# Down-projection weight tiles issued from ScalarE's DMA queue instead of SyncE's

## What is computed

```python
x = x.reshape(8, 256, 1024)          # 2048 tokens
# adapter: per batch entry, 16 ranks, indices itok_B_2_6
gate = x @ W_gate.T + 0.5 * (x @ A_gate[i].T) @ B_gate[i].T     # 2752 wide
up   = x @ W_up.T   + 0.5 * (x @ A_up[i].T)   @ B_up[i].T
act  = silu(gate) * up
down = act @ W_down.T + 0.5 * (act @ A_down[i].T) @ B_down[i].T # 1024 wide
x = x + down
x = x + (x @ weight.T + bias + scale[j] * (x @ lora_a[j].T) @ lora_b[j].T)
```

## Time and profile before

| | |
|---|---|
| time, median of 3 runs | 1600.11 us (1598.25 to 1603.44) |
| profiled execution | 1601.35 us, its span 1599.6 us |
| TensorE matmul busy | 1563.7 us, 98% |
| VectorE, GpSimd, ScalarE busy | 66%, 61%, 37% |
| TensorE's granted clock over the span | 0.995 |

### The profile page before, as it was taken

The page is one execution under the profiler, slowest core; times in us unless marked ns, Lnnn a source line. Parts: engine busy times, 40 slices in busy tenths (PEclk is TensorE's granted clock), DMA queues, the critical chain, the costliest instruction groups (busy, mean ns, idle before and its releaser), DMA issues.

```text
span 1599.6 us, 20865 instructions
## 1 busy us (share of the span) xinstructions
PE 1563.7 (98%) x6820; PEld 1275.6 (80%) x6820; DVE 1056.7 (66%) x1047; ACT 599.1 (37%) x1042; POOL 971.3 (61%) x679
## 2 busy tenths in 40 slices
PE   6999999999999999999999999999999999999998
PEld 4878888888888788888888877888787887778886
DVE  5786666666777877667677766474747546855433
ACT  3744444444445544444444422223232324431010
POOL 5577767766674777677666766767575644641110
PEclk9999999999999999999999999999999999999999
DMA  8334544533443355345552475444435242203322
GB/s 162 102 109 129 168 116 129 168 102 103 144 126 102 93 167 179 107 127 184 130 126 87 163 238 132 119 112 120 125 102 137 84 122 76 60 18 82 82 54 53
DMA packets 290878, 189.54 MB, mean 118 GB/s; under 512 B 164692, under 2 KB 252756, under 8 KB 290388
## 3 DMA queue, kind: packets, MB, share of 16 engines
q1 hardware_dynamic: 229424, 124.23, 30.7%
q10 hardware_dynamic: 61220, 63.98, 12.1%
q0 software_dynamic: 128, 0.00, 0.0%
HBM read 133.08 MB, written 56.46 MB: 118 GB/s over the span
## 4 chain that ended last, share of the span: by engine, by line
PE 85%; SPq 3%; DVE 3%; issue 3%; POOL 3%; DMA 2%; ACT 1%; DVEq 0%; ACTq 0%; POOLq 0%
PE ps L2447 85%; SPq L1477 1%; SPq L612 1%; POOL W L2223 1%; DMA x_first<-in_x_dram 1%; DMA turned_w<-in_L_cond_W_down_dram 1%; SPq L1434 1%; ACT Bf L1789 0%; DVE acc L1156 0%; DMA last_landed<-act_scratch 0%; DVE TG L663 0%; POOL Ws_S L2321 0%; POOL Bf L2306 0%; POOL act_last L2361 0%; SPq L1406 0%
## 5 line engine op out<-in xcount | busy, mean ns | idle before, releaser
L2447 PE MATMUL ps<-X_T,W 128*128 128x512 f32 x1944 | 458.0, 390 | 5.7 <-POOL W L2223 2.5
L2447 PE MATMUL ps<-X_B,W 128*128 128x512 f32 x1728 | 418.6, 392 | 14.3 <-ACT X_B L1717 13.1
L2447 PEld LDWEIGHTS ps<-X_T,W 128*128 128x128 f32 x1944 | 365.2, 188 | 84.4 <-issue 6.5
L2447 PEld LDWEIGHTS ps<-X_B,W 128*128 128x128 f32 x1728 | 326.5, 189 | 84.0 <-issue 14.6
L2223 POOL TENSOR_TENSOR W<-s,W 128x512 fp32r<-128x512 f32 x156 | 228.0, 1470 | 56.0 <-ACT W L1688 53.2
L1131 DVE TENSOR_TENSOR acc<-acc,ps 128x1024 f32<-128x1024 f32 x140 | 168.2, 1214 | 125.6 <-PE ps L2447 125.5
L2314 POOL TENSOR_TENSOR moving<-landed,moving 128x1024 fp32r<-128x1024 f32 x70 | 172.3, 2471 | 122.0 <-ACT moving L1942 122.0
L2447 PE MATMUL ps<-moving,Ws_S 128*128 128x512 f32 x960 | 222.1, 391 | 4.1 <-DVE acc L1131 2.8
L2447 PEld LDWEIGHTS ps<-moving,Ws_S 128*128 128x128 f32 x960 | 180.8, 189 | 44.0 <-issue 5.1
L2223 POOL TENSOR_TENSOR W<-TG,W 128x512 fp32r<-128x512 f32 x88 | 124.8, 1419 | 123.8 <-ACT W L1688 123.6
L1688 ACT ACTIVATE W<-s 128x512 fp32r<-128x512 f32 x156 | 98.5, 633 | 226.8 <-PE ps L2447 198.6
(11 more groups left out here) (169 smaller groups left out, 1938.3 us busy)
## 6 DMA issues: line engine op xcount, KB each, us to landing
raw<-in_L_cond_W_gate_dram SPq DMA_DIRECT2D x164, 128.0 KB, 2.9
raw<-in_L_cond_W_up_dram SPq DMA_DIRECT2D x164, 128.0 KB, 3.1
landed<-moves_scratch SPq DMA_DIRECT2D x40, 512.0 KB, 4.5
moves_scratch<-t_move ACTq DMA_DIRECT2D x60, 256.0 KB, 3.6
landed<-act_scratch SPq DMA_DIRECT2D x30, 512.0 KB, 5.3
raw<-in_x_dram SPq DMA_DIRECT2D x104, 128.0 KB, 3.5
act_scratch<-c21buf ACTq DMA_DIRECT2D x42, 256.0 KB, 2.4
turned_w<-in_L_cond_W_down_dram SPq DMA_DIRECT2D x80, 128.0 KB, 3.4
```

Source lines behind the costliest of these rows:

```text
L2447: return nc.tensor.matmul(dst, stationary, moving, start=start, stop=stop, skip_group_check=True)
```

## The change

Loading of a weight tile becomes two helpers that any engine can call, and the tiles of `b` = 1 to 4 are issued by ScalarE. They stand at the end of two steps of the first token half of the `b` before, two tiles (eight transfers) at each: `n` = 4 and 5 in `b` = 0, `n` = 1 and 2 in the others. Waits, buffers, sources and the number of transfers are the same. SyncE keeps the tiles of `b` = 0 and of the last block.

```diff
+        def down_rows(eng, buf, filled, tile):
+
+            rows = w_down.rearrange("(g i) f -> i g f", i=Q)
+            for q in range(NQ):
+                first = first_group(tile, q) * Q
+                eng.dma_start(buf[q * Q:(q + 1) * Q, :].rearrange("i (g f) -> i g f", f=Q),
+                              rows[:, :, first:first + Q]).then_inc(filled, 16)
+
+        def down_tile_load(eng, p, e):
+
+            b, j = divmod(p, 2)
+            if b == 0:
+                eng.wait_ge(spilled, 4 * 16)
+            else:
+                eng.wait_ge(ws_lo.sem, ws_lo.after((b - 1, "A22", 1)))
+            down_rows(eng, turned_w[:, j, e, :, :].rearrange("p q x -> p (q x)"), down_full[j][e], 2 * p + 1 + e)
...
             def load_sevens():
...
                 load_ad(1)
-                load_moving(6)
-                for p in (2, 3):
-                    for e in range(2):
-                        load_down(("D", p, e))
-                    load_moving(p + 5)
-                some(9, 12)
+                some(6, 12)
                 for b in range(SEVENS - 1):
                     g, p = 14 * b, 2 * b + 2
                     if b > 0:
-                        for j in range(2):
-                            for e in range(2):
-                                load_down(("D", p + j, e))
                         some(g + 7, g + 12)
...
                             if n in (2, 3):
                                 ad_high(2 * b + n - 2)
+                            if b < SEVENS - 1 and (n in (1, 2) if b else n in (4, 5)):
+                                for e in range(2):
+                                    down_tile_load(eng, 2 * b + 2 + (n - 1) % 3, e)
```

More of the change, by code:

```diff
@@ L1463, in load_down @@
                 _, bb, e = item
[L1464 to L1478, removed]
+                if bb < LAST:
+                    down_tile_load(sp, bb, e)
+                    return
+                buf, filled = slot(item)
+                down_rows(sp, buf, filled, (0, FULL)[e])
             def load_bd(item):
```

## The result

The changed kernel takes 1616.68 us (median of four), the kernel before 1600.74 us beside it. The ratio is 1.0092, with an interval of 1.0078 to 1.0105: some 15 us slower. The forecast was 1613.9 us, +13.8. One of the four executions took 2250 us at a mean clock of 0.66; it is left out of the ratio, and without it the median is 1616.09 us.

What follows compares the result with a forecast made beforehand. The prediction took TensorE, busy 98% of the span, to bound the kernel. It summed +0.5 (b = 0) + 13.5 (b = 1 to 3) - 0.2 = +13.8 us on 1600.1, giving 1613.9 us, range 1600 to 1620 us.

Steps and rivals of the forecast that it cites:

- part 1: b = 0: SyncE, without the weight transfers, issues tile 7 near 948.6; the gap before P1, costing 4.76 us, goes.
- Part 2: b = 0: ScalarE's second eight issues stand ahead of tile 8 and compete with tiles 8 to 11; net +0.5 us.
- the three cases: b = 0 outcomes: all but 0.1 of 4.76 us back; moving tiles wholly ahead, +3.1 us; queues share, +1.1 us.
- near sharing: b = 0: two queues share the DMA engines, some 4 us of moving tiles delaying the issue; +1.1 us, +0.5 taken.
- the low end: b = 0: the second eight finish in time for P5 and the old gap's cost comes back, -4.7 us.
- that far case: b = 0: moving tiles go wholly ahead of the weights, issue ends at 971.1, gap 6.1 us before P5; +3.1 us.
- Part 3: b = 1 to 3: 16 issues hold ScalarE, tile 19 is late, gap of 2.8 us at P2 plus 1.7 clock; +13.5 us.
- One sign of being wrong: b = 1 to 3: a gap already at P7, from the first eight issues taking over 6.4 us.
- Part 4: The rest: VectorE and SyncE's later tiles come sooner in b = 1 to 3, returning 0.2 us.
- A short hold: Tile 19's gap stays under about 1.5 us with full clock, or b = 0 returns 4.7; 1599.3 to 1604.5 us, chance 0.18.
- rival 2: ScalarE's issue is hardly held: no step waits in b = 1 to 3, b = 0 gains all; 1595.2 us, chance 0.07.
- the sharing case: b = 0: DMA engines alternate between the queues packet by packet, delaying the second eight and P5; +1.1 us.

Runs made afterwards that it cites:

- only_b0: Against the changed kernel, ScalarE issues only the weight tiles of b = 1 (in b = 0), SyncE keeps those of b = 2 to 4: 1603.92 us, ratio 1.0015.
- only_b123: Against the changed kernel, ScalarE issues only the tiles of b = 2 to 4 (in b = 1 to 3), b = 0 in SyncE's old order: 1611.74 us, ratio 1.0058.
- long_runs: The changed kernel with ScalarE's transfers reading 32 rows of 4 KB, not 1024 runs of 128 bytes; same bytes, other data: 1594.26 us, ratio 0.9952.

## Why the prediction was right, and where it wasn't

- **What bounds the kernel, and part 1.** Right. Tile 7 went at 949.30 (948.6 forecast; two steps of 5.44 after 937.54 are 948.4), the gap ahead of P1 is gone, and SyncE's new order gave 4.74 us back at the place where the prediction had found 4.76.
- **Part 2, `b` = 0: +0.5 us, ends -4.7 and +3.1. Wrong in size.** It cost 4.6 us in the profiled execution, outside its ends, and 2.4 by the ratio of `only_b0`, inside them. The mechanism was the one named: the second eight issues share the DMA engines with tiles 8 to 11. But the issue ended at 971.9, past the far end of the three cases (971.1), and not near sharing (969.1). Tile 12 and the adapter loads, which fall into it too, were not in that sum, and I had given weight to the low end with no row for it. The gap of that far case, 6.1 us, is what came (6.30). And the clock's price was taken from gaps of 2.4 to 2.8 us: 1.7 us. With the gap of 6.30 us it was low for some 10 us, 6 of them behind the gap, and four steps took 24.89 us and not 22.04.
- **Part 3, `b` = 1 to 3: +13.5 us.** Right in place, mechanism and order of size: 11.6 us in the trace (4.9, 4.3, 2.5), 9.3 by the ratio of `only_b123`. The gaps forecast at 2.8 are 2.59, 2.70 and 2.77; the issues, forecast to end 14.6 us after their start, ended after 14.99 in `b` = 1 (1026.79 to 1041.78). Too high was one term: the third gap, 2.77 us, brought no low clock (24 matmuls in 5.72 us), so 1.7 us fell out. The rule that a gap of over 2 us costs 1.7 us more than itself rested on two gaps of one trace, and of the 24 gaps of 2.0 to 2.9 us in the ten traces (915 to 1345 us) ten brought no low clock (last section). One sign of being wrong came true in small: the first eight in `b` = 1 took 6.66 us, over the 6.4 named, and not 5.73, which left a gap of 0.35 us at P7.
- **Part 4: -0.2 us.** About 0.9 us came back behind `b` = 3. Of it 0.56 are two small gaps of the kernel before that this one has not, 0.24 us for VectorE at 1337.02 and 0.32 for GpSimd at 1342.67. Too small to tell in the times.
- **The sum** of +13.8 against about +15 is partly luck. By the traces `b` = 0 was 4 too low and `b` = 1 to 3 were 2 too high; by the ratios of the parts run alone, 2 too low and 4 too high.
- **The rivals.** A short hold falls with the ScalarE rows: 6.66 us for eight issues that begin on idle DMA engines, 14.37 beside moving tiles. The Trainium skill's small issue time (DMA: Bandwidth & Descriptors, Issuing engines are not separate DMA queues) doesn't hold for these transfers by the same rows. It is nearer for others: in `long_runs` an issue took 0.46 us, and that run gave the -5 us and more of rival 2.

What stays open: by what rule the DMA engines choose between the two queues. The Trainium skill's alternation packet by packet (same page, Queues, rings and completion order) fits that both go on (the four moving tiles landed by 968.4, between issues of weight tiles), but no run here measured the packet. The price that the prediction had put on that rule, the sharing case with +1.1 us and an issue until 969.1, did not come out (971.9). What makes the clock come back sooner or later behind equal gaps was not tested.

## What to carry to other kernels

Before a transfer is moved to an engine with work, add up how long its issue will hold that engine, from the issue rows and not from the engine's busy share: ScalarE was busy for 37%, 16 transfers held it for 15 us, and the slack of the tile behind them was 10 us. Put issues behind the work that the next steps want, a few at a time, and keep short runs off an engine that has deadlines. And when an engine is freed, look at what it starts at once: here it was the 2 MB that held the other one.

## What the runs showed of the hardware

- The length of an issue depends on the runs and on what is under way: eight issues of weight tiles took 6.66 us when they began on idle DMA engines, 8.61 beside one moving tile and 14.37 beside five. The issues of weight tiles in the changed kernel (min/median/max ns), 64 from ScalarE, 16 from SyncE:

```profile
L630 ACTq DMA_DIRECT2D turned_w<-in_L_cond_W_down_dram x64: 318/742/4301, 949.5 to 1217.7; - x64
L630 SPq DMA_DIRECT2D turned_w<-in_L_cond_W_down_dram x16: 431/658/2144, 772.9 to 819.6; - x16
```

  The same bytes in runs of 4 KB took 0.46 us each (3.71 for eight), both times in `b` = 0.
- Issuing doesn't stop what the engine has already been given, so "it does nothing else" in the section on the profile before is too strong: tile 18's high part ran from 1033.49 to 1034.55 while the next issue had started at 1033.63. The instructions behind the issues wait.
- The granted clock behind a gap isn't a fixed price. In the changed kernel gaps of 2.59 and 2.70 us brought one low stretch each, 2.77 us none, and 6.30 us one of 10 us. A gap of 2.75 us ahead of P6 in `b` = 0 stands in the traces of all kernels, where no edit touches it: P6 took 7.16 us behind it in the kernel before and 5.69 in the changed one.
